# A two-layer graph network on one core: four relations' projections around one x per table row, projected in row halves, with x laid out by partition

## The reference, cut to what matters

```python
# x (12500, 64); src, dst, etype (400000,), dst sorted; efeat (400000, 64); relation_weight (32, 64, 64)
h_proj = einsum('nd,rde->rne', x, relation_weight)
att = sum(h_proj[etype, src] * tanh(h_proj[etype, dst] + efeat), -1)
a = exp(att - segment_max(att, dst)[dst]); a = a / segment_sum(a, dst)[dst]
h_nb = segment_sum(x[src] * a[:, None], dst)
y = layernorm(x + leaky_relu((x + h_nb) @ w1.T) + leaky_relu(x * h_nb @ w2.T))
z = segment_sum((y / out_degree)[src], dst) / in_degree
out = layernorm(y + z)
```

## Time and profile before

| | us |
|---|---|
| median of 3 runs | 12504.19 |
| the profiled execution | 12504.09 |
| its span in the profile | 12502.3 |
| POOL busy | 9106.9 (73%) |
| DVE busy | 4974.7 (40%) |
| ACT busy | 2167.4 (17%) |
| PE busy | 1355.6 (11%) |
| stage 1 ends, stage 2 begins | 406.1 |
| first node gather, stage 3 | 8250.7 |

### The profile page before, as it was taken

How to read it: one execution, slowest core, us unless ns; L and a number is a source line. 1 busy time by engine, 2 the same in 40 slices (tenths; PEclk the granted TensorE clock), 3 DMA queues, 4 the chain that set the end, 5 groups by cost and what they waited for, 6 DMA issues and landing times. The chain is left out here.

```text
span 12502.3 us, 36138 instructions
## 1 busy us (share of the span) xinstructions
PE 1355.6 (11%) x4902; PEld 711.9 (6%) x4902; DVE 4974.7 (40%) x4627; ACT 2167.4 (17%) x1796; POOL 9106.9 (73%) x9773
## 2 busy tenths in 40 slices
PE   9311111110101111111111111140000000000001
PEld 3100000000000000000000000040000000000001
DVE  4455555555555555555555555561111111111113
ACT  4111111111111111111111111122222222222221
POOL 1577777777777777777777777757777777777776
PEclk9655555555555555555555555555555555555555
DMA  9422222222222222222222222211222222222222
GB/s 403 174 80 79 79 79 79 80 79 80 79 80 79 80 79 79 79 79 79 79 79 79 79 79 79 77 41 51 53 52 53 52 53 53 52 53 52 53 52 50
DMA packets 456359, 998.94 MB, mean 80 GB/s; under 512 B 189300, under 2 KB 242276, under 8 KB 443412
## 3 DMA queue, kind: packets, MB, share of 16 engines
q0 software_dynamic: 356272, 519.14, 18.2%
q1 hardware_dynamic: 62004, 271.05, 5.6%
q10 hardware_dynamic: 38064, 208.54, 4.2%
HBM read 629.48 MB, written 368.55 MB: 80 GB/s over the span
## 5 line engine op out<-in xcount | busy, mean ns | idle before, releaser
L1044 POOL DMA_INDIRECT gy<-ytab,idx x3125 | 2948.3, 943 | 999.6 <-issue 952.1
L817 POOL DMA_INDIRECT gs<-table,idx_s x3125 | 2953.3, 945 | 971.3 <-issue 971.3
L820 POOL DMA_INDIRECT gd<-table,idx_d x3125 | 2948.0, 943 | 951.3 <-issue 951.3
L1077 DVE TENSOR_TENSOR_SCAN run<-keep,add 128x1664 f32<-128x1664 f32 x125 | 452.9, 3623 | 3015.1 <-ACT keep L1101 3015.1
L868 DVE TENSOR_TENSOR banks<-banks,gd 128x1600 f32<-128x1600 f32 x125 | 229.0, 1832 | 3430.4 <-DMA gd<-table,idx_d 3430.4
L1006 PE MATMUL banks<-hi,lo 128*128 128x392 bf16 x3125 | 803.4, 436 | 6984.7 <-DVE hi L855 6984.7
L855 DVE TENSOR_TENSOR hi<-banks,digit 128x9800 bf16<-128x9800 f32 x125 | 1294.3, 10354 | 0.0
L972 ACT ACTIVATE banks<-banks 128x1600 f32<-128x1600 f32 x125 | 186.0, 1488 | 4912.5 <-DVE banks L868 4912.5
L1099 ACT COPY add<-gy 128x1600 f32<-128x1600 f32 x125 | 400.4, 3203 | 2474.2 <-DMA gy<-ytab,idx 2474.2
L1006 PEld LDWEIGHTS banks<-hi,lo 128*128 128x128 bf16 x3125 | 381.4, 126 | 7406.7 <-DVE hi L855 7033.6
L982 ACT COPY rowbuf<-run 128x1625 f32<-128x1625 f32 x125 | 410.2, 3282 | 776.4 <-DVE run L895 776.4
(11 more groups left out here) (184 smaller groups left out, 2402.7 us busy)
## 6 DMA issues: line engine op xcount, KB each, us to landing
table<-rows SPq DMA_DIRECT2D x98, 1536.0 KB, 9.4
sums<-rowbuf ACTq DMA_DIRECT2D x125, 825.0 KB, 3.7
ef<-in_edge_attr_dram SPq DMA_DIRECT2D x125, 800.0 KB, 4.9
sums<-rowbuf ACTq DMA_DIRECT2D x125, 800.0 KB, 3.5
gs<-table,idx_s POOLq DMA_INDIRECT x3125, 2.6
gd<-table,idx_d POOLq DMA_INDIRECT x3125, 2.4
gy<-ytab,idx POOLq DMA_INDIRECT x3125, 2.4
ytab<-y SPq DMA_DIRECT2D x7, 448.0 KB, 3.5
```

The source lines that it names most:

```text
L817: pool.indirect_dma_start(out=gs[:, s, g, :], out_offset=None, in_=table, in_offset=bass.IndirectOffsetOnAxis(ap=idx_s[:, s, g:g + 1], axi ...
L820: pool.indirect_dma_start(out=gd[:, s, g, :], out_offset=None, in_=table_third, in_offset=bass.IndirectOffsetOnAxis(ap=idx_d[:, s, g:g + 1 ...
L1044: pool.indirect_dma_start(out=gy[:, s, g, :], out_offset=None, in_=ytab, in_offset=bass.IndirectOffsetOnAxis(ap=idx[:, s, g:g + 1], axis=0 ...
L1077: nc.vector.tensor_tensor_scan(run[:, :, :].rearrange("p w t -> p (w t)"), keep[:, :, :].rearrange("p w t -> p (w t)"), add[:, :, :].rearr ...
```

## The change

A table row now holds four relations' projections with one x in the middle: P0, P1, x, P2, P3, five vectors of 64 floats, 8 rows to a node. The gather by `src` still takes three vectors, starting at vector 0 or 2 of the row, so that x is the third or the first of them; an edge's type gives three flags, `odd`, `right` and `left`, that pick the projection, and x is moved to one place by a predicated copy whose mask lies in PSUM (`side`). The projection contracts over 64 rows only, with the weights of the even pairs in partitions 0 to 63 and those of the odd pairs in 64 to 127, in alternation. In stage 1 a node goes to partition node // 98, so that each partition's part of x is one run in DRAM, and each store goes to 128 regions of the table. Only the first 50 entries of the edge lists are loaded in stage 1; the rest, and x once more in the old layout, are loaded in stage 2. Several tiles are no longer cleared.

```diff
-        table = nc.dram_tensor("table", (NPAD * R // 2, 3 * D), F32).ap()
+        table = nc.dram_tensor("table", (NPAD * R // 4, 5 * D), F32).ap()
...
-        table_third = table.rearrange("a (b d) -> (a b) d", b=3)
+        table_vec = table.rearrange("a (b d) -> (a b) d", b=5)
...
+        SOON = 2 * G
+        src_v, dst_v, type_v = (v.rearrange("(p t) -> p t", p=P) for v in (src, dst, etype))
...
             nc.vector.tensor_scalar(odd[:, s, :], type_sb[:, at], 1, None, ALU.bitwise_and)
+            nc.vector.tensor_scalar(quad[:, :], type_sb[:, at], 2, None, ALU.logical_shift_right)
             link.then(nc.vector.tensor_scalar(half[:, :], type_sb[:, at], 1, None, ALU.logical_shift_right))
-            nc.vector.scalar_tensor_tensor(out=idx_s[:, s, :], in0=src_sb[:, at], scalar=float(R // 2),
-                                           in1=half[:, :], op0=ALU.mult, op1=ALU.add)
-            link.then(nc.vector.scalar_tensor_tensor(out=place[:, :], in0=type_sb[:, at], scalar=2.0,
-                                                     in1=half[:, :], op0=ALU.mult, op1=ALU.subtract))
-            nc.vector.scalar_tensor_tensor(out=idx_d[:, s, :], in0=dst_sb[:, at_d], scalar=float(3 * R // 2),
+            nc.vector.tensor_scalar(right[:, s, :], half[:, :], 1, None, ALU.bitwise_and)
+            nc.vector.scalar_tensor_tensor(out=near[:, :], in0=half[:, :], scalar=2.0, in1=quad[:, :], op0=ALU.mult, op1=ALU.add)
+            link.then(nc.vector.scalar_tensor_tensor(out=place[:, :], in0=type_sb[:, at], scalar=1.0,
+                                                     in1=half[:, :], op0=ALU.mult, op1=ALU.add))
+            nc.vector.tensor_scalar(left[:, s, :], right[:, s, :], 0, None, ALU.is_equal)
+            link.then(nc.vector.scalar_tensor_tensor(out=place[:, :], in0=quad[:, :], scalar=-1.0,
+                                                     in1=place[:, :], op0=ALU.mult, op1=ALU.add))
+            nc.vector.scalar_tensor_tensor(out=idx_s[:, s, :], in0=src_sb[:, at], scalar=float(5 * R // 4),
+                                           in1=near[:, :], op0=ALU.mult, op1=ALU.add)
+            nc.vector.scalar_tensor_tensor(out=idx_d[:, s, :], in0=dst_sb[:, at_d], scalar=float(5 * R // 4),
                                            in1=place[:, :], op0=ALU.mult, op1=ALU.add).then_inc(slot_ready, 1)
...
-            POOL_DUP, ACT_DUP = 4, 4
-            RP = R // 2
-            FIRST = 4
-            w_all = sb(c1, "w_all", [P, R, D])
-            rows = sb(c1, "rows", [P, SLOTS, RP, 3 * D])
+            POOL_DUP, ACT_DUP = 2, 2
+            FIRST, RQ = 4, R // 4
+            w_all = sb(c1, "w_all", [P, RQ, 2, D])
+            rows = sb(c1, "rows", [P, SLOTS, RQ, 5 * D])
...
-            x_zero, w_zero = sem(c1, "x_zero"), sem(c1, "w_zero")
+            x_zero = sem(c1, "x_zero")
+            x_by_part = x[0:(P - 1) * NB, :].rearrange("(p b) d -> p b d", b=NB)
+            table_by_part = table.rearrange("(p b r) c -> p b (r c)", p=P, b=NB)
...
-                    engine.wait_ge(x_first, 16)
+                    engine.wait_ge(x_first, 32)
...
+                    sp.dma_start(xs[0:P - 1, 0:FIRST, :], x_by_part[:, 0:FIRST, :]).then_inc(x_first, 16)
+                    sp.dma_start(xs[P - 1:P, 0:FIRST, :], x[(P - 1) * NB:(P - 1) * NB + FIRST, :].unsqueeze(0)).then_inc(x_first, 16)
                     sp.wait_ge(x_zero, 1)
-                    sp.dma_start(xs[:, 0:FIRST, :], x[0:FIRST * P, :].rearrange("(b j) d -> j b d", j=P)).then_inc(x_first, 16)
-                    sp.dma_start(xs[0:TAILROWS, NB - 1, :], x[(NB - 1) * P:N, :]).then_inc(x_in, 16)
-                    sp.dma_start(xs[:, FIRST:NB - 1, :], x[FIRST * P:(NB - 1) * P, :].rearrange("(b j) d -> j b d", j=P)).then_inc(x_in, 16)
+                    sp.wait_ge(w_in, 64)
+                    sp.dma_start(xs[0:P - 1, FIRST:, :], x_by_part[:, FIRST:, :]).then_inc(x_in, 16)
+                    sp.dma_start(xs[P - 1:P, FIRST:N - (P - 1) * NB, :], x[(P - 1) * NB + FIRST:N, :].unsqueeze(0)).then_inc(x_in, 16)
                     sp.wait_ge(idx_pad, 5)
-                    sp.dma_start(src_sb[:, 0:T], src.rearrange("(p t) -> p t", p=P)).then_inc(idx_in, 16)
-                    sp.dma_start(dst_sb[:, 1:1 + T], dst.rearrange("(p t) -> p t", p=P)).then_inc(idx_in, 16)
+                    sp.dma_start(src_sb[:, 0:SOON], src_v[:, 0:SOON]).then_inc(idx_in, 16)
+                    sp.dma_start(dst_sb[:, 1:1 + SOON], dst_v[:, 0:SOON]).then_inc(idx_in, 16)
+                    sp.dma_start(type_sb[:, 0:SOON], type_v[:, 0:SOON]).then_inc(idx_in, 16)
                     with nc.allow_non_contiguous_dma(reason="one number of each partition"):
                         sp.dma_start(head_next[0:P - 1, :], dst[T:E].rearrange("(p t) -> p t", p=P - 1)[:, 0:1]).then_inc(idx_in, 16)
-                    sp.dma_start(type_sb[:, 0:T], etype.rearrange("(p t) -> p t", p=P)).then_inc(idx_in, 16)
 
                     def store(b, s, i):
                         sp.wait_ge(dup_ready, b + 1)
                         for k in range(4):
                             sp.wait_ge(taken[k], b + 1)
-                        sp.dma_start(table[bass.ds(b * P * RP, P * RP), :].rearrange("(j r) c -> j (r c)", r=RP),
-                                     rows[:, s, :, :].rearrange("p r c -> p (r c)")).then_inc(stored[s], 16)
+                        sp.dma_start(table_by_part[:, bass.ds(b, 1), :],
+                                     rows[:, s:s + 1, :, :].rearrange("p o r c -> p o (r c)")).then_inc(stored[s], 16)
 
                     each_block(sp, store, False)
...
-                        pool.tensor_copy(rows[:, s, RP - POOL_DUP:RP, D:2 * D],
+                        pool.tensor_copy(rows[:, s, RQ - POOL_DUP:RQ, 2 * D:3 * D],
...
-                    pe.wait_ge(w_zero, 1)
-                    pe.wait_ge(w_in, 16)
+                    pe.wait_ge(w_in, 64)
...
-                            nc.tensor.matmul(ps_p[k][:, :], xbT[:, s, :],
-                                             w_all[:, k * R // 4:(k + 1) * R // 4, :].rearrange("d r e -> d (r e)"),
+                            u, h = k // 2, k % 2
+                            nc.tensor.matmul(ps_p[k][:, :], xbT[64 * h:64 * h + D, s, :],
+                                             w_all[64 * h:64 * h + D, 4 * u:4 * u + 4, :, :].rearrange("d q c e -> d (q c e)"),
                                              start=True, stop=True).then_inc(proj_ready[k], 1)
 
...
-                    copy(rows[:, s, k * RP // 4:(k + 1) * RP // 4, :].rearrange("p q (c e) -> p q c e", c=3)[:, :, 0:3:2, :],
-                         ps_p[k][:, :].rearrange("p (q c e) -> p q c e", c=2, e=D)).then_inc(taken[k], 1)
+                    q0, e0 = k // 2 * RQ // 2, k % 2 * 3 * D
+                    copy(rows[:, s, q0:q0 + RQ // 2, e0:e0 + 2 * D],
+                         ps_p[k][:, :].rearrange("p (q e) -> p q e", e=2 * D)).then_inc(taken[k], 1)
...
-                    nc.vector.memset(xs[:, NB - 1, :], 0.0).then_inc(x_zero, 1)
-                    nc.vector.memset(w_all[D:P, :, :], 0.0).then_inc(w_zero, 1)
+                    nc.vector.memset(xs[96:P, N - (P - 1) * NB:, :], 0.0).then_inc(x_zero, 1)
                     nc.vector.memset(src_sb[:, T:], 0).then_inc(idx_pad, 1)
...
-                        nc.vector.tensor_copy(rows[:, s, 0:RP - POOL_DUP - ACT_DUP, D:2 * D],
-                                              xs[:, bass.ds(b, 1), :].to_broadcast([P, RP - POOL_DUP - ACT_DUP, D]))
+                        nc.vector.tensor_copy(rows[:, s, 0:RQ - POOL_DUP - ACT_DUP, 2 * D:3 * D],
+                                              xs[:, bass.ds(b, 1), :].to_broadcast([P, RQ - POOL_DUP - ACT_DUP, D]))
...
-                    act.dma_start(w_all[0:D, :, :], rel_w.rearrange("r d e -> d r e")).then_inc(w_in, 16)
+                    w_v = rel_w.rearrange("(q h c) d e -> h c d q e", h=2, c=2)
+                    for h in range(2):
+                        for k in range(2):
+                            act.dma_start(w_all[64 * h:64 * h + D, :, k, :], w_v[h, k]).then_inc(w_in, 16)
...
+            side = banks[:, 7, D:D + G].bitcast(I32)
...
                     load(0, 0)
+                    sp.dma_start(src_sb[:, SOON:T], src_v[:, SOON:]).then_inc(rest_in, 16)
+                    sp.dma_start(dst_sb[:, 1 + SOON:1 + T], dst_v[:, SOON:]).then_inc(rest_in, 16)
+                    sp.dma_start(type_sb[:, SOON:T], type_v[:, SOON:]).then_inc(rest_in, 16)
                     load(1, 1)
+                    sp.wait_ge(x_pad, 1)
+                    sp.dma_start(xs[:, 0:NB - 1, :], x[0:(NB - 1) * P, :].rearrange("(b j) d -> j b d", j=P)).then_inc(x_again, 16)
+                    sp.dma_start(xs[0:TAILROWS, NB - 1, :], x[(NB - 1) * P:N, :]).then_inc(x_again, 16)
...
+                    sp.wait_ge(x_again, 32)
...
-                                out=gs[:, s, g, :], out_offset=None, in_=table,
```

(43 more changed lines are left out.)

22 lines of the change are left out of this document (13 added, 9 removed).

## The result

| | us |
|---|---|
| changed kernel, median of 8 runs | 12541.43 (12540.9 to 12542.43) |
| kernel before beside it, median of 8 | 12503.15 (12502.03 to 12504.48) |
| ratio | 1.0031, 95% interval 1.0022 to 1.0039 |
| its profiled execution, span | 12542.43, 12540.6 |

The change makes the kernel 38.3 us slower. 12535 was forecast, with 12526 to 12546 as the range of the sum itself.

A forecast was written before the change was run, and what follows sets the result against it. DMA engines bound at most the first 400 us; the rest is a count of gathers, unchanged. Stage 1 +25.8 us and the end of stage 2 +5.0, total +30.8 on 12504.09, gave 12535 us, range 12526 to 12546.

The forecast's parts named there:

- The x load: Stage 1: 127 partitions go through one DMA engine, 113.7 us from about 10, so x is in at 124.
- SP: Stage 1, SP's queue: blocked again behind the 127-row `head_next` load, so the first table store goes at 124 us.
- The stores' pace: Stage 1: 98 smaller table stores at 3.084 us each, 308 us from first store to next stage.
- PE: Stage 1 projections: the array's two halves run at once, some 2.2 us a block, hidden under stores of 3.08.
- rival of PE as the bound: Stage 1: halves do not overlap, 49 us more (12575), or the clock falls, about 12630; chance 0.18.
- DVE in the loop: Stage 2 loop: some 7 us more DVE work a chunk, hidden under 62.5 us of gathers; costs nothing.
- clears: Start of stage 2 and the mean stage: POOL does not wait for DVE's clears, so dropping them gains nothing.
- gathers: From stage 2 on: exactly as many gathers with the same row sizes, still 944 ns each; no change.
- The lists' 11 us: Stage 1: most of the edge lists, 4.7 MB, leave it, taking 11 us of DMA from the front.
- The end of stage 2: Behind the last gather: DVE's bare chain gets a product, reduction and predicated copy, less index operations; +5.0 us.
- rival of the spread x: Stage 1: x load spread over all engines, 7.5 us, stage 1 ends at 323, 83 earlier, total 12426; chance 0.15.

The follow-up runs named there:

- full-row run: The cut kernel with every projection over all 128 rows instead of 64: 13921.74 us against 13964.15 for the kernel before (ratio 0.997), stage 2 at 366.34.
- cut kernel: The changed kernel with both 127-row x loads cut into 112 + 15 rows: 13880.18 us against 13953.42 for the kernel before (ratio 0.9947).
- 124 + 3 cut: The changed kernel with each 127-row x load cut into 124 and 3 rows: 13912.85 us against 13953.42 for the kernel before (ratio 0.9971).

## Why the prediction was right

Slower was given 0.70, and the mechanism was the forecast's. By its own terms:

- **The x load: right.** One engine, a share of 0.07 for 0.06, issued at 10.77 for 10. It was in at 126.9 for 124: the issue came 0.8 us later, and 10 + 113.7 left out some 2 us from the issue to the first piece and behind the last. The 112 + 15 cut shows this term alone: 104.4 us.
- **SP: right.** I let SP be held behind `head_next` and the first store go at 124. It was held inside the issue of the first store, right behind `head_next`, until 126.49, and no piece of the table moved earlier. What I had not seen is that every issue from 11.05 on would be held, not that one alone.
- **The stores' pace: the mis-sized term.** 98 x 3.084 + 5.7 = 308 us was forecast, at 425 GB/s. From x in to stage 2 it took 440.0 - 126.9 = 313.1, which is 98 x 3.19 + 0.5. So the pace took 10.4 us more than I gave it, and the 5.7 set aside for it and for latency covered about half, by luck rather than by a reading. The error was made in the trace of the kernel before: I took the 425 of the earlier trace rows for the pace, where its blocks followed each other at 3.79 us, 415 GB/s, in that stretch as in all others. 5/6 of 3.79 would have been 3.16. Five of the eight microseconds that stage 1 is over the forecast (33.9 against 25.8) lie here, three in x. The placing of the table has no part in it; why the smaller pieces go 1% slower is open.
- **PE: right.** The halves overlap, 1.99 us a block for the 1.8 I took, clock 1.00. The rival of PE as the bound was priced too high where serial: 30.7 us by the full-row run, not 49, since the stores are slower than I took them and a full-row block takes 3.55 us, not 3.60. Serial within one half it would have been far worse, 414.5 us, which I had not foreseen.
- **DVE in the loop, clears, gathers: right,** each at nothing here (5.6 us more DVE work a chunk for the 7 I took). The lists' 11 us stood in no sum of mine. In the cut kernel they measured 11.3; what they would be in the changed kernel no run shows.
- **The end of stage 2: +4.4 for +5.0.** The product took 1.81 for 1.83, the reduction 1.81 for 1.75, and the predicated copy, which I had put at 1.7 between 0 and 3.5, 1.92. These make 5.5; they add less to the path, since parts of them lie under their neighbours and under ACT's exponentials, and the index operations at the end are gone.

On the profiled executions the time rose by 38.3 where the sum was 30.8: 8.1 us too little for stage 1, 0.6 too much for the end of stage 2. The rival of the spread x, 83 us earlier for stage 1, was not what happened, but the cut kernel made it so, and its stage 2 began at 335.65 where I had said 323: again the stores' pace, and x in at 22.6, 16 us after its issue and not 7.5, by the slower pieces.

## What to carry to other kernels

Look at the number of partitions of every large load before its layout or its bytes: 127 partitions in one load cost 104 us here, and cutting it into 112 + 15 gave a kernel 73 us faster than the one before, where the change as it is lost 32 on the same kind of chip. In a window without work, a DMA share of one sixteenth says so at a glance. And look at where a wait stands. The wait for x stood ahead of the stream of stores and not beside it, so it was added whole, and the savings behind it counted in full in both kernels. Stage 1 of the cut kernel is 70.5 us shorter than before: 98 x (3.79 - 3.19) = 59 by the smaller stores, for which the row halves are needed (31 of them), and 11 by the late lists. The changed kernel has the same stream, 313.1 us from x in to stage 2 for 313.0, and 104.4 us ahead of it. Last, a pace is read from how steps follow each other, not from the GB/s of one window.

## What I had not expected of the hardware

- **PE at half pace for a whole stage, and a clock record that does not say so.** With all projections in rows 0 to 63, pieces took 0.90 us and the full transposition 477 ns for the whole of stage 1, though PE was busy for 100 of 100 us. One projection in four in the other half brought 0.45 and some 310. The record read 1.00, as it does in every trace here until its first fall, PE's slow first block included; durations of an unedited instruction showed the pace. What keeps the pace down isn't shown.
- **Large pieces slow each other.** A piece of 24,064 bytes of x took 0.90 us when one engine read alone (0.07 of 16 engines, 28 GB/s). With four engines the window's share of 0.24 at 66 GB/s gives 0.24 x 16 x 24,064 / 66,000 = 1.40 us a piece, and with sixteen it was 1.47, 247 GB/s in all, where the table's stores reach 411. That is why the 124 + 3 cut came 12 us after its forecast. Its cause was not tried.
- **The gathers' price differs between chips**: 944 ns a gather where the change was measured, 1035 to 1100 where the experiments ran, and the kernel before takes 13942 to 13964 us instead of 12503, while stage 1 of the changed kernel agrees to 0.3 us.
